# Skip rows of a graph kernel made in the output stage from the loaded destination rows, in place of in the messages

## The reference

```
m = x @ W_n2m.T                       # 256 -> 128
q, k, v = m @ Wq.T + bq, m @ Wk.T + bk, m @ Wv.T + bv      # 4 heads of 32
e = (edge_attr @ W_edge.T) @ We.T
alpha = softmax over the edges of a destination of (q[dst] * (k[src] + e)).sum * scale
out = segment_sum((v[src] + e) * alpha, dst)               # 128 wide
x_r = m @ Wskip.T + bskip
beta = sigmoid([out, x_r, out - x_r] @ Wbeta.T)
y = (beta * x_r + (1 - beta) * out) @ W_m2n.T
x = layernorm(x + y)
```

## Time and profile before

| | |
|---|---|
| median of 3 runs | 1362.51 us (1362.12 to 1378.24) |
| profiled execution | 1371.76 us |
| its span, first to last instruction | 1370.0 us |
| mean granted clock of TensorE | 0.958 |
| TensorE products busy | 1198.5 us (87%) |
| VectorE busy | 1045.4 us (76%) |
| POOL busy | 838.7 us (61%) |
| ScalarE busy | 808.2 us (59%) |

### The profile page before, as it was taken

One profiled execution on the slowest core, in us unless ns is written; L12 is line 12 of the kernel. 1 busy time (PEld: TensorE's weight loads), 2 busy tenths in 40 slices (PEclk: granted clock), 3 DMA queues, 4 the chain that ended last, 5 costly groups with the idle time before them and its releaser, 6 DMA issues. The chain is left out here.

```text
span 1370.0 us, 28397 instructions
## 1 busy us (share of the span) xinstructions
PE 1198.5 (87%) x7186; PEld 1044.4 (76%) x7186; DVE 1045.4 (76%) x3775; ACT 808.2 (59%) x2683; POOL 838.7 (61%) x1044
## 2 busy tenths in 40 slices
PE   3799999999996799899898699999999994788881
PEld 2688898988895677777776699999999993566660
DVE  3476676776679798889787788888888877788781
ACT  0366565665567765666556466666666667365562
POOL 4688888888743455455444566666666643267675
PEclk9899999999999999999999899999999998799995
DMA  6668889888763487887777766667666642556541
GB/s 157 196 184 260 261 257 273 269 273 266 233 199 121 142 248 237 242 247 240 221 238 208 221 199 196 199 185 211 197 191 204 195 129 78 161 180 185 174 156 57
DMA packets 208937, 277.05 MB, mean 202 GB/s; under 512 B 40060, under 2 KB 140563, under 8 KB 208777
## 3 DMA queue, kind: packets, MB, share of 16 engines
q1 hardware_dynamic: 188793, 224.13, 53.2%
q0 software_dynamic: 19264, 50.85, 12.9%
q10 hardware_dynamic: 720, 0.26, 0.1%
HBM read 159.73 MB, written 117.12 MB: 202 GB/s over the span
## 5 line engine op out<-in xcount | busy, mean ns | idle before, releaser
L743 PE MATMUL banks<-m_ext,node_XT 128*128 128x257 f32 x1568 | 379.9, 385 | 0.0
L743 PEld LDWEIGHTS banks<-m_ext,node_XT 128*128 128x128 f32 x1568 | 288.2, 194 | 33.7
L769 DVE SCALAR_TENSOR_TENSOR node_X<-banks,node_be,node_X 128x256 f32<-128x256 f32 x392 | 169.8, 475 | 83.9 <-ACT node_be L695 69.8
L670 POOL TENSOR_TENSOR node_r<-node_vv,half 128x4 f32<-128x4 f32 (+1 forms) x202 | 214.6, 1062 | 17.2 <-POOL node_vv L665 0.3
L701 ACT ACTIVATE node_XT<-banks 128x512 f32<-128x512 f32 x196 | 117.1, 598 | 143.7 <-PE banks L733 137.5
L665 POOL TENSOR_SCALAR node_vv<-node_mv 128x4 f32<-128x4 f32 (+1 forms) x202 | 57.6, 285 | 223.7 <-DVE node_mv L777 207.2
L762 DVE BATCH_NORM_STATS2 node_st<-node_X 128x6 f32<-128x256 f32 x392 | 145.8, 414 | 17.4 <-DMA node_X<-in_x 16.1
L708 ACT ACTIVATE node_sq<-node_X 128x256 f32<-128x256 f32 x392 | 157.9, 408 | 0.0
L733 PE MATMUL banks<-ident,node_X 128*128 128x128 f32 x784 | 123.6, 281 | 30.1 <-DVE node_X L783 15.1
L682 ACT ACTIVATE node_X<-node_X,node_r 128x256 f32<-128x256 f32 x326 | 145.9, 496 | 1.4 <-POOL node_r L670 1.4
L733 PEld LDWEIGHTS banks<-ident,node_X 128*128 128x128 f32 x784 | 96.7, 150 | 43.0 <-issue 20.1
(11 more groups left out here) (265 smaller groups left out, 2730.6 us busy)
## 6 DMA issues: line engine op xcount, KB each, us to landing
node_X<-in_x SPq DMA_DIRECT2D x196, 256.0 KB
out<-node_X SPq DMA_DIRECT2D x196, 256.0 KB
ring<-rows SPq DMA_DIRECT2D x210, 128.0 KB
rows<-ring SPq DMA_DIRECT2D x100, 256.0 KB
rows<-ring SPq DMA_DIRECT2D x200, 128.0 KB
MB<-keeps SPq DMA_DIRECT2D x40, 320.0 KB, 5.4
store<-rows SPq DMA_DIRECT2D x90, 128.0 KB
MB<-picks SPq DMA_DIRECT2D x50, 128.0 KB
```

The costliest lines, as they stand in the source:

```text
L670: pool.tensor_tensor(r[:, s % 4, NT * lo:NT * hi], v, self.c.half[:, NT * lo:NT * hi], ALU.pow).then_inc(self.roots, 1)
L743: last = pe.matmul(ps[:, NT * o + k, 0:D + 1], self.XT[:, o, k * D + h * P:k * D + (h + 1) * P], c.m_ext[:, h, :], start=(h == 0), stop=(h ...
L769: last = dve.scalar_tensor_tensor(out=X[:, n % U, k, :], in0=ps[:, b + k, 0:D], scalar=self.be[:, n % 4, k:k + 1], in1=X[:, n % U, k, :], ...
```

## The change

The messages no longer make or keep skip rows. The output stage turns the loaded destination row (two transposes into bank 6), ScalarE copies it out of PSUM, adding one, and TensorE multiplies it by `m_ext`. The matrix `w_out1` gets two more columns, wa and minus wa, so the aggregate's product gives its part of the logit with both signs; ScalarE copies these two numbers (`part`), and they enter the sigmoids as bias. MSG is transposed into bank 5 alone, and after the products of the row. The loads of rows wait for `made` in place of `product`.

```diff
@@ Message
-                at_least(pe, self.x_kept, n)
                 at_least(pe, self.q_used, n)
-                for h in range(2):
-                    pe.matmul(ps[:, 7, DM:2 * DM], c.w_qs[:, h, DM:2 * DM], c.ST[:, o, (2 + h) * P:(3 + h) * P], start=(h == 0), stop=(h == 1))
...
-                act.wait_ge(self.q_product, n + 1)
-                act.activation(c.store[:, n, DM:2 * DM], ps[:, 7, DM:2 * DM], ACT.Copy).then_inc(self.x_kept, 1)
...
-                dve.wait_ge(self.x_kept, n + 1)
+                dve.wait_ge(self.q_product, n + 1)
@@ Output, sync
                 if n >= self.HELD:
-                    sp.wait_ge(self.product, n - self.HELD + 1)
+                    sp.wait_ge(self.made, n - self.HELD + 1)
@@ Output, tensor
             if live(t, 0, TILES):
-                pe.wait_ge(self.made, t + 1)
-                at_least(pe, self.scanned, t - 1)
-                pe.transpose(ps[:, 5 + t % 2, 0:P], c.MSG[:, t % G, 0:DM], c.ident[:, :]).then_inc(self.turned, 1)
+                pe.wait_ge(self.rows_in[t % self.M], self.rows_before[t % self.M] + 16 * (t // self.M + 1))
+                at_least(pe, self.zt_ready, t)
+                for h in range(2):
+                    last = pe.transpose(ps[:, 6, h * P:(h + 1) * P], self.row(t)[:, h * P:(h + 1) * P], c.ident[:, :])
+                last.then_inc(self.z_turned, 1)
             if live(t, 2, TILES):
                 n = t - 2
-                agg, skip = self.PAIRS[n % 3]
+                skip = self.PAIRS[n % 3][1]
                 if n == 0:
                     pe.wait_ge(self.nodes.updated, NSTEPS)
+                pe.wait_ge(self.zt_ready, n + 1)
+                at_least(pe, self.z_ready, n - 2)
+                for h in range(2):
+                    pe.matmul(ps[:, skip, 0:D + 1], self.ZT[:, n % 4, h * P:(h + 1) * P], c.m_ext[:, h, :], start=(h == 0), stop=(h == 1))
+            if live(t, 0, TILES):
+                pe.wait_ge(self.made, t + 1)
+                at_least(pe, self.scanned, t)
+                pe.transpose(ps[:, 5, 0:P], c.MSG[:, t % G, 0:DM], c.ident[:, :]).then_inc(self.turned, 1)
+            if live(t, 2, TILES):
+                n = t - 2
                 pe.wait_ge(self.scanned, n + 1)
-                at_least(pe, self.z_ready, n - 2)
-                pe.matmul(ps[:, skip, 0:D + 1], c.store[:, n, DM:2 * DM], c.w_out1[:, :], start=True, stop=True)
-                pe.matmul(ps[:, skip, D:D + 1], self.AG[:, n % 5, :], c.wa[:, :], start=False, stop=True, skip_group_check=True)
-                pe.matmul(ps[:, agg, 0:D], self.AG[:, n % 5, :], c.w_out1[:, 0:D], start=True, stop=True).then_inc(self.product, 1)
+                pe.matmul(ps[:, self.PAIRS[n % 3][0], 0:D + 3], self.AG[:, n % 5, :], c.w_out1[:, :], start=True, stop=True).then_inc(self.product, 1)
@@ Output, scalar
                 act.wait_ge(self.product, n + 1)
+                at_least(act, self.gates_ready, n - 2)
+                act.activation(self.part[:, n % 3, :], ps[:, self.PAIRS[n % 3][0], D + 1:D + 3], ACT.Copy).then_inc(self.parted, 1)
+            if live(t, 0, TILES):
+                act.wait_ge(self.z_turned, t + 1)
+                at_least(act, self.product, t - 3)
+                act.activation(self.ZT[:, t % 4, :], ps[:, 6, 0:D], ACT.Copy, bias=1.0).then_inc(self.zt_ready, 1)
+            if live(t, 3, TILES):
+                n = t - 3
+                act.wait_ge(self.parted, n + 1)
                 at_least(act, self.z_ready, n - 2)
                 logit = ps[:, self.PAIRS[n % 3][1], D:D + 1]
-                act.activation(self.gates[:, n % 3, 0:1], logit, ACT.Sigmoid, scale=-1.0)
-                act.activation(self.gates[:, n % 3, 1:2], logit, ACT.Sigmoid).then_inc(self.gates_ready, 1)
+                act.activation(self.gates[:, n % 3, 0:1], logit, ACT.Sigmoid, scale=-1.0, bias=self.part[:, n % 3, 1:2])
+                act.activation(self.gates[:, n % 3, 1:2], logit, ACT.Sigmoid, bias=self.part[:, n % 3, 0:1]).then_inc(self.gates_ready, 1)
```

More of the change, by code:

```diff
@@ L256 @@
     HEADS_READY, NODES_READY, ALL_READY = 1, 2, 3
-    SPREAD, FUSED, MIXED = 19, 24, 27
+    SPREAD, FUSED, MIXED = 20, 25, 28
     def __init__(self, nc, c, ctx):
@@ L305, in emit @@
                 for k in range(2):
-                    pe.matmul(ps[:, 3 + k, 0:D + 1], w.w_skipn[:, k * P:(k + 1) * P], c.w_out1[:, :], start=True, stop=True)
-                pe.matmul(ps[:, 7, 0:D + 1], w.bs_cols, c.w_out1[:, :], start=True, stop=True).then_inc(self.pe_done, 1)
+                    pe.matmul(ps[:, 3 + k, 0:D + 1], w.w_skipn[:, k * P:(k + 1) * P], c.w_out1[:, 0:D + 1], start=True, stop=True)
+                pe.matmul(ps[:, 7, 0:D + 1], w.bs_cols, c.w_out1[:, 0:D + 1], start=True, stop=True).then_inc(self.pe_done, 1)
             if s == 4:
@@ L351, in emit @@
                 own(dve.tensor_scalar(w.bs_cols[:, 1:P], w.zero[:, 1:P], w.bs_cols[:, 0:1], None, ALU.add))
-                own(dve.tensor_copy(c.wa[:, :], w.wa))
+                own(dve.tensor_copy(c.w_out1[:, D + 1:D + 2], w.wa))
+                own(dve.tensor_scalar(c.w_out1[:, D + 2:D + 3], w.wa, -1.0, None, ALU.mult))
                 assert own.n == self.SPREAD
@@ L1280, in __init__ @@
         self.attrs = [sem(f"attrs{k}") for k in range(2)]
-        self.padded, self.counted, self.measured, self.widened, self.roots, self.normed, self.a_turned, self.et_ready, self.turned, self.zt_ready, self.q_product, self.kv_product, self.x_kept, self.k_kept, self.v_kept, self.q_used, self.scored = (
-            sem(n) for n in ("padded", "counted", "measured", "widened", "roots", "normed", "a_turned", "et_ready", "turned", "zt_ready", "q_product", "kv_product", "x_kept", "k_kept", "v_kept", "q_used", "scored"))
+        self.padded, self.counted, self.measured, self.widened, self.roots, self.normed, self.a_turned, self.et_ready, self.turned, self.zt_ready, self.q_product, self.kv_product, self.k_kept, self.v_kept, self.q_used, self.scored = (
+            sem(n) for n in ("padded", "counted", "measured", "widened", "roots", "normed", "a_turned", "et_ready", "turned", "zt_ready", "q_product", "kv_product", "k_kept", "v_kept", "q_used", "scored"))
         self.into = c.rows1.rearrange("(t p) d -> t p d", p=P)
@@ L1287, in scored_by @@
         pe.wait_ge(self.v_kept, TILES)
-        pe.wait_ge(self.x_kept, TILES)
     def all_kept(self, eng):
@@ L1510, in __init__ @@
         self.gates = sb("gates", [P, 3, 2])
+        self.part = sb("part", [P, 3, 2])
         self.sq = c.ST[:, :, 0:D]
+        self.ZT = c.AT_flat[:, 0:4 * D].rearrange("p (a n) -> p a n", a=4)
         self.va = sb("va", [P, 3, max(GROUPS)])
@@ L1517, in __init__ @@
         self.keeps = [sem(f"keeps{k}") for k in range(2)]
-        self.made, self.turned, self.scanned, self.gates_ready, self.halfway, self.product, self.z_ready, self.squared, self.widened, self.roots, self.y_ready = (
-            sem(n) for n in ("made", "turned", "scanned", "gates_ready", "halfway", "product", "z_ready", "squared", "widened", "roots", "y_ready"))
+        self.made, self.turned, self.scanned, self.z_turned, self.zt_ready, self.parted, self.gates_ready, self.halfway, self.product, self.z_ready, self.squared, self.widened, self.roots, self.y_ready = (
+            sem(n) for n in ("made", "turned", "scanned", "z_turned", "zt_ready", "parted", "gates_ready", "halfway", "product", "z_ready", "squared", "widened", "roots", "y_ready"))
         self.rows_v = c.rows1.rearrange("(t p) d -> t p d", p=P)
@@ L1635, in emit @@
                 carry = self.AG[:, (t - 1) % 5, EDGES:EDGES + 1] if t > 0 else 0.0
-                dve.tensor_tensor_scan(self.AG[:, t % 5, :], c.MB[:, t // G % 2, t % G, :], ps[:, 5 + t % 2, 0:P], carry, ALU.mult, ALU.add).then_inc(self.scanned, 1)
+                dve.tensor_tensor_scan(self.AG[:, t % 5, :], c.MB[:, t // G % 2, t % G, :], ps[:, 5, 0:P], carry, ALU.mult, ALU.add).then_inc(self.scanned, 1)
             if live(t, 4, TILES):
@@ L1774, in build @@
         c.we2 = sb("we2", [P, 2, DM])
-        c.wa = sb("wa", [P, 1])
-        c.w_out1 = sb("w_out1", [P, D + 1])
+        c.w_out1 = sb("w_out1", [P, D + 3])
         c.half = sb("half", [P, 2 * NT])
```

## The result

| | before | changed |
|---|---|---|
| median, first chip | 1362.43 us (4 runs, 1362.12 to 1378.24) | 1394.59 us (4 runs, 1392.59 to 1399.56) |
| ratio | | 1.0221, 95% interval 1.0151 to 1.029 |
| profiled execution | 1371.76 us, span 1370.0 | 1395.9 us, span 1394.1 |

The kernel became 32.2 us slower: 2.2%, with 2% inside the interval. The forecast was 1410 us, 47.5 slower.

A forecast was written before the change was run, and what follows sets the result against it. TensorE bounds the messages; in the output stage, where no engine is full, a serial chain across engines would bind after the change. Messages -32, output +79, tail and stage start +1 give +48 on 1362.5: 1410 us, range 1370 to 1450.

The forecast's parts named there:

- The circle: Output stage: MSG transpose, scan, second gate product and row products run in series, 2.24 us a tile against 1.65 before.
- The messages: Message stage: without skip products and copy, 3.26 us a tile, -32 us in all, ends -45 and 0.
- The products taken out: Message stage: the four TensorE instructions of L1388 that go, priced at 0.45 us a tile.
- The wait for the skip copy: Message stage: VectorE's idle wait at L1438, 24.0 us in 300, to become a wait for the q product, some 0.3 us earlier.
- The late results: Output stage: TensorE results arriving late, cause unknown, taken as 0.2 us a tile on top of 2.24, giving 2.44.
- TensorE's own sum: Output stage: TensorE's instructions alone, 0.22 + 0.95 + 0.19 + 0.52 = 1.88 us a tile.
- rival A: Output stage: TensorE's own work binds at 1.88 us a tile, late results hidden, messages gain 45; 1341 us; chance 0.09.
- Tail: Scatters at the end, paced by POOL, have less of a queue at a slower beat: 0 to -4 us.
- start of the stage: Output stage: its start at half clock costs 0 to +5 us; with the end of the scatters +1 together.
- The loads of rows: Output stage: the moved loads cost nothing, with ten steps = 22 us of lead left.
- rival C: Output stage falls to half clock for good, step 3.3 us, +165 - 32, 1495 us; chance 0.06.

The follow-up runs named there:

- e1: Changed kernel with the two skip products, ScalarE's copy and its semaphore put back into the messages, the rows unused: 1406.52 us.
- changed again: The changed kernel, unchanged, run on another chip beside the kernel before: 1396.7 us, ratio 1.018 to the kernel before.
- e2: Changed kernel with TensorE's MSG transpose moved ahead of the row's transposes and products in each output step: 1313.37 us, ratio 0.988 to the kernel before.
- e3: Changed kernel with VectorE's second gate product moved ahead of the scan in each output step: 1315.71 us, ratio 0.9899 to the kernel before.
- e4: Kernel before without the two skip products, ScalarE's copy and its semaphore, skip part left out: 1296.58 us, ratio 0.9744 to the kernel before.
- b_again: The kernel before, unchanged, run again with a profile beside the changed kernel on another chip: 1377.22 us, ratio 1.0037.
- e8: Kernel before without the scatters of the rows from the eleventh tile on, most output left out: 1303.55 us, ratio 0.979 to the kernel before.
- e9: Kernel before with POOL's power of the root replaced by a product of the same shape: 1316.79 us, ratio 0.9902 to the kernel before.

## Why the prediction was right, and where it was off

**The circle.** The step that decided the sign was right in kind and size: transpose, scan, second gate product, row products in series, 2.24 forecast, 2.25 to 2.26 measured, in each of the three profiles that have the circle (changed, e1, and changed again). e2 and e3 each open it at another link and both fall to 1.64 to 1.66. That the aggregate's product and the next row's transposes are hidden beside it was right too.

**The messages.** Forecast -32, measured -35.4 in the profiles and -32.9 by e4. I took 3.26 us a tile where 3.28 came out of 3.64. (I had 3.58 for the start: I divided the length by 100 tiles instead of 99 distances, which gives 3.62, and took it at L1388; at L1367 it is 3.64.) The busy shares came out near: TensorE at 99.0% where I expected less than 98%, VectorE at 94% where I expected over 93%. (I called 3.26 "96% of both"; for VectorE, 3.05 of 3.26 is 94%.) The products taken out were priced at 0.45 us and gave 0.36. Among the rest are TensorE's waits for VectorE, longer than before but still short, as I had assumed. The wait for the skip copy went from 24.0 to 0.0 us as forecast.

**The late results.** This is the term that was mis-sized: "I take 0.2, near to what they cost today: 2.44 us a tile". They cost 2.34 - 2.25 = 0.09 in the changed kernel, and the output stage +68.4 us instead of +79. I thought that a late result of 1.5 to 2 us would stand in the circle in full. It was 0.5 to 0.6 us, once in five tiles from tile 34 on, and there was none in e1. Why it shrank no run shows; that about 0.2 was taken and not 0 or 0.5 was a guess, and that the term stayed small is luck as much as judgement. With 0.09 in place of 0.2, the sum would have been 1399.

**TensorE's own sum.** 1.88 forecast for rival A, 1.64 shown by e2: spacings taken from a step in which TensorE waited are not its work. It didn't enter the forecast. With it, rival A would have read 1362.5 - 35 - 0 = 1327 us for an opened order on the first chip, an estimate from the steps of e2.

**The rest.** Tail -1.0, start of the stage -0.3: forecast +1 together. The loads of rows and ScalarE's copies set no pace that shows: ScalarE was 70% busy, and the quiet step is the circle's links alone. The clock: the row of 1165 to 1367 us has the granted clock at 1.00, the 2.4 GHz level, with TensorE 79% busy and two more transposes in each step than the earlier trace rows with 0.95. The rule of the Trainium skill (TensorE: Matmul & The Clock Gate, Part 4: PE-mode transpose), that transposes don't count as activity the way products do, spoke for rival C; this trace shows no drop from them.

## What to carry to other kernels

Before work is moved to a place ahead of a wait, follow one tile's semaphores once around all engines, and count in how many steps the chain closes. A circle that closes within one step costs its whole length in each step, though no engine is full; the remedy is an order, not less work. For the work of an engine take spacings from a stretch in which it is full, never from one in which it waits.

## What the runs showed of the hardware

The same kernel before had medians of 1329 and 1331 us beside two groups of runs and of 1362 and 1374 us at two other times, and the cost of the change came out as 32 us in the first comparison, 23 to 25 in the second (not clear of each other) and some 44 by the sum of steps on a fast chip. The quiet output steps were equal to 0.01 us on all (1.36 and 2.26); what differed was the earlier part of the program (messages begin at 742 to 747 us in the profiles of the fast chips, at 756 to 776 in the others) and the long steps.

In the kernel before, results of TensorE reached VectorE and ScalarE up to 2 us late (2.25 us idle ahead of the scan of 1319.62, b_again), at a cost of 0.11 (e4) to 0.36 us a tile (b_again). They were on time without the indirect scatters (1.37 us a tile, e8) and with a product in place of the power on POOL (1.36, e9, its scatters still 1.28 us apart), and in the reordered kernel e2 with power and scatters in place.
